# First attention: query and key norms by logarithm, exponential and a Newton step, and key norms moved into the softmax exponential

## What is computed

```python
xn = ln(x, g_norm)
q = heads(xn @ Wq)                       # 16 heads of 64
k, v = split(xn @ Wkv)                   # one head of 64, null key and value put in front
q = l2norm(q) * q_scale                  # l2norm(t) = t / max(norm(t), 1e-12)
k = l2norm(k) * k_scale
sim = q @ k.T * 8 + bias                 # bias: a small network of the relative position; causal mask
out = ln(softmax(sim) @ v @ Wout, g_out)
```

## Time and profile before

| | us |
|---|---|
| median of three runs (251.5 to 252.31) | 252.21 |
| the profiled execution | 251.66 |
| its span in the trace | 249.9 |
| GpSimd busy, 75 instructions | 58.4 |
| ScalarE busy, 178 instructions | 122.1 |
| VectorE busy, 360 instructions | 162.8 |
| TensorE busy, 1906 matmuls | 210.8 |

### The profile page before, as it was taken

The page is one execution under the profiler, slowest core; times in us unless marked ns, Lnnn a source line. Parts: engine busy times, 40 slices in busy tenths (PEclk is TensorE's granted clock), DMA queues, the critical chain, the costliest instruction groups (busy, mean ns, idle before and its releaser), DMA issues.

```text
span 249.9 us, 4768 instructions
## 1 busy us (share of the span) xinstructions
PE 210.8 (84%) x1906; PEld 141.4 (57%) x1906; DVE 162.8 (65%) x360; ACT 122.1 (49%) x178; POOL 58.4 (23%) x75
## 2 busy tenths in 40 slices
PE   0188798478897899999979989997889999999992
PEld 0154364343453464547356655764556899999992
DVE  2888779819148386889858975973953745474424
ACT  0216497677364255371634347538666542553230
POOL 3605949990000001200410027020003012000000
PEclk9999999999999999999999999999999999999997
DMA  6910055000003503400530070000000000000000
GB/s 187 422 44 0 0 146 199 4 1 0 3 0 63 129 3 107 84 0 3 116 77 0 24 155 16 0 3 0 3 3 1 4 0 21 3 21 0 21 0 21
DMA packets 10068, 11.75 MB, mean 47 GB/s; under 512 B 928, under 2 KB 9648, under 8 KB 9792
## 3 DMA queue, kind: packets, MB, share of 16 engines
q1 hardware_dynamic: 10048, 11.47, 16.5%
HBM read 10.38 MB, written 1.09 MB: 46 GB/s over the span
## 4 chain that ended last, share of the span: by engine, by line
PE 52%; DVE 27%; ACT 8%; POOL 5%; issue 4%; DMA 2%; DVEq 0%; SPq 0%; ACTq 0%
PE banks L1671 13%; PE banks L1376 6%; PE banks L1730 5%; DVE probs L958 5%; PE banks L1343 4%; PE banks L1271 3%; PE banks L1478 3%; PE banks L1396 2%; PE banks L1419 2%; PE banks L1438 2%; DMA rows<-in_rows 2%; ACT probs L594 2%; DVE zin L975 2%; ACT probs L556 2%; PE banks L1404 2%
## 5 line engine op out<-in xcount | busy, mean ns | idle before, releaser
L958 DVE TENSOR_TENSOR probs<-probs,eb 128x1024 f32<-128x1024 f32 x24 | 28.7, 1209 | 17.9 <-ACT probs L556 17.9
L594 ACT ACTIVATE probs<-banks,shift 128x1024 f32<-128x1024 f32 x24 | 25.9, 1112 | 14.9 <-PE banks L1461 14.7
L556 ACT ACTIVATE probs<-banks,key_shift 128x1024 f32<-128x1024 f32 x24 | 25.9, 1112 | 12.0 <-PE banks L1343 11.5
L1343 PE MATMUL banks<-qt,kT 64*128 64x512 f32 x96 | 25.4, 628 | 2.6 <-ACT probs L556 2.1
L1376 PE MATMUL banks<-probs,kvt 128*64 128x512 f32 (+1 forms) x128 | 23.3, 496 | 3.7 <-DVE probs L958 3.4
L363 POOL TENSOR_TENSOR qin<-qss,minus_half 128x16 f32<-128x16 f32 x8 | 23.1, 2903 | 6.4 <-DVE qss L797 6.3
L356 POOL TENSOR_TENSOR ve<-mv,ln_eps 128x2 f32<-128x2 f32 x4 | 1.7, 428 | 82.6 <-DVE mv L985 82.6
L1376 PEld LDWEIGHTS banks<-probs,kvt 128*64 128x64 f32 x128 | 7.8, 137 | 16.9 <-issue 9.7
L1671 PE MATMUL banks<-keys_space,wb 128*128 128x256 f32 (+1 forms) x72 | 17.3, 381 | 0.0
L1271 PE MATMUL banks<-wa,on 128*128 128x512 f32 x32 | 16.1, 628 | 1.2 <-DVE spread L803 1.2
L1203 DVE SCALAR_TENSOR_TENSOR x<-banks,ga,x 128x96 f32<-128x96 f32 (+1 forms) x32 | 10.2, 318 | 10.2 <-PE banks L1730 7.4
(11 more groups left out here) (214 smaller groups left out, 424.2 us busy)
## 6 DMA issues: line engine op xcount, KB each, us to landing
spread<-softmax_inverse_sums SPq DMA_DIRECT2D x16, 256.0 KB, 5.9
eb<-bias_table SPq DMA_DIRECT2D x4, 512.0 KB, 5.9
wb<-in_wb SPq DMA_DIRECT2D x1, 1842.0 KB, 10.5
wa<-in_wa SPq DMA_DIRECT2D x1, 1160.0 KB, 7.0
x<-in_x SPq DMA_DIRECT2D x1, 512.0 KB, 3.8
softmax_inverse_sums<-zin SPq DMA_DIRECT2D x4, 128.0 KB, 1.7
out<-x SPq DMA_DIRECT2D x4, 128.0 KB, 1.8
rows<-in_rows SPq DMA_DIRECT2D x1, 456.0 KB, 5.6
```

The lines of the kernel that those rows point to most:

```text
L556: nc_.activation(pb[c], sc[:, 1024 * (c % 2):1024 * (c % 2 + 1)], ACT.Exp, bias=key_shift[:, b, k:k + 1]).then_inc(s["exp_done"], 1)
L594: nc_.activation(pb[c], sc[:, 1024 * SLOT[c]:1024 * (SLOT[c] + 1)], ACT.Exp, bias=shift2[:, 3:4]).then_inc(s["exp2_done"], 1)
L958: v.tensor_tensor(p, p, w, ALU.mult).then_inc(s["mult_done"], 1)
L1343: last = mm(out.rearrange("p (m i) -> p m i", m=rhs.shape[1]), lhs, rhs, start=True, stop=True)
```

## The change

The power of -0.5 of the query tiles 3 to 7 is replaced by a logarithm and an exponential on ScalarE (`query_roots`, now there) and a Newton step of four instructions on GpSimd (`query_newton`). The key norms are made in the same way (`key_roots`, `key_newton`); the keys themselves are no longer multiplied by them: GpSimd copies the raw keys twice side by side (`keys_doubled`), and the inverse norm becomes the per-partition scale of the exponentials in `weights` and `extra_weights`. `keys_out` moves from ScalarE to VectorE. The two table loads of the stage are replaced by one, behind the last raw copy. The order of the work of all four engines is written out anew: TensorE turns the first two batches of keys ahead of query tile 5 and the other two behind the first scores, which wait for one batch instead of four, and ScalarE copies tile 7 behind the first exponential. The names of new semaphores are left out of the diff.

```diff
@@ -365,6 +366,33 @@
             def query_roots(t):
                 inverse_roots(qss[:, t], qin[:, t], "qss_ready", t, "qinv_ready")
 
+            steps = [0]
+
+            def newton(ss, root, once, done):
+
+                def then(ins):
+                    steps[0] += 1
+                    ins.then_inc(s["root_step"], 1)
+                    pool.wait_ge(s["root_step"], steps[0])
+
+                then(pool.tensor_tensor(once, root, root, ALU.mult))
+                then(pool.tensor_tensor(once, once, ss, ALU.mult))
+                then(pool.tensor_scalar(once, once, -0.5, 1.5, ALU.mult, ALU.add))
+                pool.tensor_tensor(root, root, once, ALU.mult).then_inc(s[done], 1)
+
+            def query_newton(t):
+                pool.wait_ge(s["query_roots"], t - 2)
+                pool.wait_ge(s["qinv_ready"], t)
+                newton(qss[:, t], qin[:, t], q_once[:], "qinv_ready")
+
+            def key_newton():
+                pool.wait_ge(s["key_roots"], 1)
+                newton(kss[:], kin[:], ksr[:], "kinv_ready")
+
+            def keys_doubled():
+                pool.wait_ge(s["kvt_ready"], B)
+                pool.tensor_copy(kn, kvt[:].rearrange("p b t c -> p (b t) c")[:, :, None, 0:DH].to_broadcast([P, 3 * B, 2, DH])).then_inc(s["kn_ready"], 1)
+
             def later_windows(g):
                 pool.wait_ge(s[f"windows_loaded_{g}"], 32)
                 pool.tensor_copy(eb1[:, :, 4 * g:4 * g + 4], eb0[:, :, 4 * g:4 * g + 4, 0:P]).then_inc(s["windows_copied"], 1)
@@ -378,13 +406,17 @@
                 pool.memset(buf[:], 0.0)
             pool.memset(zeros[:], 0.0).then_inc(s["cleared"], 1)
             rstd(bmv[:, :, 1], ln_eps, bve[:], brs[:], s["bias_var"], s["bias_rstd"], s["bias_pool"], 1)
-            for t in range(5):
+            for t in range(3):
                 query_roots(t)
+            keys_doubled()
+            query_newton(3)
+            query_newton(4)
+            key_newton()
+            query_newton(5)
             later_windows(0)
-            query_roots(5)
+            query_newton(6)
             later_windows(1)
-            query_roots(6)
-            query_roots(7)
+            query_newton(7)
 
             def last_normalised():
                 b = B - 1
@@ -458,18 +490,16 @@
                 nc_.activation(ksq, kvt[:].rearrange("p b t c -> p (b t) c")[:, :, 0:DH], ACT.Square).then_inc(s["ksq_ready"], 1)
 
             def key_roots():
-                nc_.preload_act_table(ACT.Sqrt)
                 act.wait_ge(s["kss_ready"], 1)
-                nc_.activation(ksr[:], kss[:], ACT.Sqrt).then_inc(s["ksr_ready"], 1)
-
-            def keys_out(b):
-                act.wait_ge(s["k_turned"], b + 1)
-                at = 512 * (b % 2)
-                nc_.activation(kT[:, b], oa[:, at:at + 2 * P], ACT.Copy, scale=qk_scale[:, 0:1])
-                for e in range(2):
-                    r = slice(DH * e, DH * (e + 1))
-                    last = nc_.activation(kx[r, b, e], oa[r, at + 2 * P:at + 2 * P + 2], ACT.Copy, scale=qk_scale[r, 0:1])
-                last.then_inc(s["kt_ready"], 1)
+                nc_.activation(kin[:], kss[:], ACT.Ln).then_inc(s["key_logs"], 1)
+                act.wait_ge(s["key_logs"], 1)
+                nc_.activation(kin[:], kin[:], ACT.Exp, scale=-0.5).then_inc(s["key_roots"], 1)
+
+            def query_roots(t):
+                act.wait_ge(s["qss_ready"], t + 1)
+                nc_.activation(qin[:, t], qss[:, t], ACT.Ln).then_inc(s["query_logs"], 1)
+                act.wait_ge(s["query_logs"], t - 2)
+                nc_.activation(qin[:, t], qin[:, t], ACT.Exp, scale=-0.5).then_inc(s["query_roots"], 1)
 
             def query_squares(t):
                 act.wait_ge(s["q_proj"], t + 1)
@@ -498,27 +528,30 @@
             keys_values_raw(2)
             keys_values_tokens(2)
             keys_values_raw(3)
+            nc_.preload_act_table_set("natural_log_exp_and_others")
             keys_values_tokens(3)
             bias_table()
             query_squares(3)
+            key_norms()
             queries_out(0)
-            key_norms()
+            query_roots(3)
             query_squares(4)
             queries_out(1)
+            query_roots(4)
+            query_squares(5)
             key_roots()
-            query_squares(5)
             queries_out(2)
-            nc_.preload_act_table_set("natural_log_exp_and_others")
+            query_roots(5)
             query_squares(6)
             queries_out(3)
+            query_roots(6)
             query_squares(7)
             queries_out(4)
             queries_out(5)
-            for b in range(B):
-                keys_out(b)
+            query_roots(7)
             queries_out(6)
-            queries_out(7)
             act.wait_ge(s["shifts"], 1)
+            act.wait_ge(s["kinv_ready"], 1)
 
             def group_read(i):
 
@@ -554,14 +587,14 @@
                     act.wait_ge(s["z_done"], 2 * b - 1 + c // 3)
                 k = c % 3 // 2
                 nc_.activation(pb[c], sc[:, 1024 * (c % 2):1024 * (c % 2 + 1)], ACT.Exp,
-                               bias=key_shift[:, b, k:k + 1]).then_inc(s["exp_done"], 1)
+                               bias=key_shift[:, b, k:k + 1], scale=kin[:, b, k:k + 1]).then_inc(s["exp_done"], 1)
 
             def extra_weights(b):
                 act.wait_ge(s["qk_x"], b + 1)
                 if b:
                     act.wait_ge(s["z_done"], 2 * b)
                 nc_.activation(px[0:2], mb[0:2, 0:32].rearrange("p (e m q) -> p e m q", e=2, m=M), ACT.Exp,
-                               bias=key_shift[0:2, b, 2:3]).then_inc(s["px_exp"], 1)
+                               bias=key_shift[0:2, b, 2:3], scale=kin[0:2, b, 2:3]).then_inc(s["px_exp"], 1)
 
             def evacuate(b, g):
                 act.wait_ge(s["pv_done"], 2 * b + g + 1)
@@ -570,6 +603,7 @@
                 nc_.copy(ob[b % 2][:, 4 * g:4 * g + 4], halves(oa, 4)).then_inc(s["o_evac"], 1)
 
             weights(0, 0)
+            queries_out(7)
             weights(0, 1)
             extra_weights(0)
             for b in range(B):
@@ -780,14 +814,14 @@
                 dve.wait_ge(s["kss_raw"], 1)
                 v.tensor_scalar(part, part, 1e-24, None, ALU.max).then_inc(s["kss_ready"], 1)
 
-            def keys_scaled():
-
-                dve.wait_ge(s["ksr_ready"], 1)
-                v.reciprocal(kin[:], ksr[:]).then_inc(s["kinv_ready"], 1)
-                dve.wait_ge(s["kinv_ready"], 1)
-                n = 3 * B
-                v.tensor_tensor(kn, kvt[:].rearrange("p b t c -> p (b t) c")[:, :, None, 0:DH].to_broadcast([P, n, 2, DH]),
-                                kin[:].rearrange("p b t -> p (b t)")[:, :, None, None].to_broadcast([P, n, 2, DH]), ALU.mult).then_inc(s["kn_ready"], 1)
+            def keys_out(b):
+                dve.wait_ge(s["k_turned"], b + 1)
+                at = 512 * (b % 2)
+                v.tensor_scalar(kT[:, b], oa[:, at:at + 2 * P], qk_scale[:, 0:1], None, ALU.mult)
+                for e in range(2):
+                    r = slice(DH * e, DH * (e + 1))
+                    last = v.tensor_scalar(kx[r, b, e], oa[r, at + 2 * P:at + 2 * P + 2], qk_scale[r, 0:1], None, ALU.mult)
+                last.then_inc(s["kt_ready"], 1)
 
             def query_sums(t):
 
@@ -882,17 +916,20 @@
             queries_scaled(1)
             query_sums(3)
             queries_scaled(2)
-            key_sums()
             query_sums(4)
             queries_scaled(3)
+            key_sums()
             query_sums(5)
             queries_scaled(4)
-            keys_scaled()
             query_sums(6)
             queries_scaled(5)
+            queries_scaled(6)
             query_sums(7)
-            queries_scaled(6)
+            keys_out(0)
+            keys_out(1)
             queries_scaled(7)
+            keys_out(2)
+            keys_out(3)
 
 
             dve.wait_ge(s["bias_loaded"], 16 * 8)
@@ -1319,9 +1356,9 @@
             turn_queries(3)
             queries(7)
             turn_queries(4)
+            turn_keys(0)
+            turn_keys(1)
             turn_queries(5)
-            for b in range(B):
-                turn_keys(b)
             turn_queries(6)
 
 
@@ -1421,8 +1458,10 @@
                 last.then_inc(s["qkv_done"], 1)
 
             pe.wait_ge(s["qt_ready"], T)
-            pe.wait_ge(s["kt_ready"], B)
+            pe.wait_ge(s["kt_ready"], 1)
             scores(0, 0)
+            turn_keys(2)
+            turn_keys(3)
             turn_queries(7)
             scores(0, 1)
             extra_scores(0)
```

More of the change, by code:

```diff
@@ L154, in adaln_ffn @@
         qin = sb("qin", [P, B * T, H])
+        q_once = sb("q_once", [P, H])
         qt = sb("qt", [P, B, M, S])
@@ L239, in adaln_ffn @@
             bias_top table_ready table_stored windows_loaded_0 windows_loaded_1 windows_copied bias_loaded
```

(4 more changed lines are left out.)

## The result

| | before | after |
|---|---|---|
| median, us (4 executions each, timed together) | 251.99 | 248.87 |
| ratio of the times, 95% interval | | 0.988 (0.986 to 0.991) |
| span of the profiled execution, us | 249.9 | 246.6 |
| first product with the values (the mark), us | 60.24 | 56.42 |

The forecast was 249.3, with 248.1 to 251.3 as its range.

The account below looks back on a forecast made before the run. Bound: a chain of waits through tile 7's root on GpSimd. Steps of -3.5 plus 0.49 give -3.0 at the mark; +0.4 after makes -2.6, 251.66 to 249.05; half-way to the median, 249.3 us; range 248.1 to 251.3.

Parts of the forecast that it names:

- to the end of tile 7's sums: VectorE's sums of query tile 7 end at 47.6 us, practically as before: -0.05 us.
- sums to scaling (the root): From tile 7's sums to its scaling, with logarithm, exponential and four GpSimd steps for a power: 3.43 to 1.8 us, -1.63.
- scaling of tile 7 to its turn: Wait for tile 7's turn on TensorE, shorter as first scores want one key batch, not four: 2.2 to 1.3 us, -0.9.
- its turn to the mark: Tile 7's turn to first product with values, first exponential and multiply done beside tile 7's copy: 7.0 to 6.05, -0.95.
- supplement for the layout: The hand-made schedule of the kernel before put the mark at 59.75, trace 60.24; this 0.49 us was added to the new one.
- mark to the end: After the first product with the values, four exponentials on the chain each 0.09 us longer: nearly +0.4 us.
- the GpSimd step: One 128x16 Newton instruction on GpSimd: estimated 0.22 us, four steps and three gaps 1.1 us; from 0.45 the gain is lost.
- the load: ScalarE's table load behind the last raw copy, 1.28 us; rival 2.66 with drain gives 250.4 to 250.7, chance 0.06 with bias table.
- the second operand: The per-partition scale added to each first-attention exponential on ScalarE: 0.09 us more each; rival with all 24 on path 0.05.
- blocked GpSimd steps: Rival: each GpSimd Newton step waits out a VectorE instruction, 1.1 us a step; time about 265 us, chance 0.04.
- The held clamp: VectorE's clamp held by a GpSimd window copy: costs up to 0.9 us of tile 6, 250 to 250.5 us.
- The multiply with the bias table: Rival: row loads start late, so VectorE's first multiply waits 1.2 us: 250.3 to 251 us, chance 0.06 with long load.

Follow-up runs that it names:

- roots_alone: The kernel before with only the new roots and the one early table load, keys multiplied on VectorE and old order kept: 254.23 us, 1.008 of the kernel before.
- newton_out: The changed kernel without the Newton steps of keys and queries: 249.46 us, 0.991 of the kernel before.
- order_better: The changed kernel with squares of tiles 4 and 6 earlier, tile 7's sums ahead of tile 6's scaling, last keys turned later: 249.87 us, 0.992 of the kernel before.
- power_kept: The changed kernel with the roots of query tiles 3 to 7 as powers on GpSimd again: 255.19 us, 1.013 of the kernel before.
- keys_first: The changed kernel with all four key batches turned ahead of tile 6 and the first scores waiting for all four: 252.01 us, 1.002 of the kernel before.

## Why the prediction was right

The steps of the sum, each from the traces of before and after, counted from the maximum over the bias table:

| step | before | after | measured | predicted |
|---|---|---|---|---|
| to the end of tile 7's sums | 18.50 | 18.54 | +0.04 | -0.05 |
| sums to scaling (the root) | 3.43 | 1.89 | -1.54 | -1.63 |
| scaling of tile 7 to its turn | 2.18 | 1.48 | -0.70 | -0.9 |
| its turn to the mark | 6.98 | 5.89 | -1.09 | -0.95 |
| supplement for the layout | | | | +0.49 |
| to the mark | 31.09 | 27.80 | -3.29 | -3.0 |
| mark to the end | 189.66 | 190.18 | +0.52 | +0.4 |

The turn of tile 7 is taken from the chain both times (53.26 in the earlier trace rows, 50.53 above). The first two steps came out within 0.1 us and the other two within 0.2, these two together within 0.1. The supplement was twice what it should have been: it took the layout to fall as far short after as before, 0.49, and after it fell short by 0.24, the sum of the four errors. All in all the traces give 2.77 less where 2.6 was forecast, and 251.66 less 2.77 is 248.89. That this is so close is in part luck, since the supplement was 0.25 too large and the stretch behind the mark 0.12 longer than forecast, and the two offset each other. That the point was put half-way to the median of before, at 249.3, can't be judged by the times: the same changed kernel had medians of 248.87 and 249.74.

The costs behind these steps held too: the GpSimd step 0.20 to 0.22 (estimate 0.22), the load 1.28 without a drain, the second operand 0.09. After the mark the estimate counted four exponentials on the path; 0.52 came, but removing the operand gave back only 0.22 there, so 0.3 of it is something else, which stays open. Of the rivals, blocked GpSimd steps had no case: none of the twenty of 128x16 was near 0.45. By the rule of the Trainium skill (GPSIMD Engine Reference, section 1, Specifications) this rival had no place in the stage; the steps agree. roots_alone shows what the move of the key multiply avoids. There the multiply, of two SBUF inputs, stays on VectorE, and a GpSimd step beside it takes 1.68 us for 0.20 and ends with it (VectorE's row, then GpSimd's):

```profile
42.62 1.75 DVE L826 TENSOR_TENSOR probs<-kvt,kin 128x1536 f32<-128x1536 f32 x1
```

```profile
42.75 1.68 POOL L380 TENSOR_SCALAR q_once<-q_once 128x16 f32<-128x16 f32 x1
```

Nothing waited for that step, but it is what the rival described. The held clamp, priced at up to 0.9, did not come up in after (46.99, 0.17 us), though it did in two of the experiments. The multiply with the bias table waited for no load: it followed VectorE's last key copy without a pause, at 52.00, 0.93 us after the end of the first exponential (49.86 + 1.21).

Two things the prediction did not see. What is late next, once the root has left the path, is TensorE's order of turns and scores together with ScalarE's copies; newton_out shows that a still shorter root gives nothing. And the gain is not a sum over parts that could be had one by one. The new roots in the old order gain nothing, and the new order with the old roots loses time, each by its own waits and then by the clock that TensorE can lose in them. The layout by hand reckons with a full clock, and the profile after has one, as in the earlier trace rows; where the clock fell, in three of the experiments, the same layout was off by 0.9 to 1.8 us. The prediction holds no word on what the new order does to the clock, so that it stayed full was luck as far as the working goes. The clock isn't the only thing that the layout can miss: for order_better it was off by 1.3 us at the full clock.

## What to carry to other kernels

Follow a late tile by hand through every engine's list to one mark, in the old and in the new order, and compare mark with mark from an event ahead of the change: that told tenths of a microsecond where the times told one. When a long serial step is shortened, ask which engine's order becomes the path, since a further shortening was worth nothing here. Read TensorE's granted clock by short stretches whenever a reordering makes it wait: work placed into those waits was worth more here than its own duration.

## What was not expected of the hardware

- **The clock falls inside a kernel's stage.** In power_kept, roots_alone and keys_first TensorE went to a granted clock of 0.50 after it had been busy 1.76 of 4 us, not at all in 2 us, and 1.90 of 4 us, and its next pieces took 1.47 to 2.08 us for 0.85 to 1.13. It came back to 1.00 as TensorE worked on. The same kernel can show the fall in one execution and not in the next (roots_alone).
- **A copy or memset on GpSimd holds a small VectorE instruction.** The clamp of 128x16 takes 0.17 us. In order_better it took 0.45 (45.59), and ended with a window copy on GpSimd (44.97 + 1.04). In newton_out it ended with a memset of 128x4096 on GpSimd, which stood earlier there than in after (44.57 + 3.52 = 48.09). VectorE of newton_out:

```profile
47.25 0.87 DVE L826 TENSOR_SCALAR qss<-qss 128x16 f32<-128x16 f32 x1
47.33 0.79 DVE L815 TENSOR_SCALAR kT<-banks,qk_scale 128x256 f32<-128x256 f32 x1
```

The key copy shown behind it waits for it (0.79, otherwise 0.48). In after the same memset runs from 50.31 to 53.83, and the key copies beside it, which read PSUM, keep their 0.48, and the first multiply with the bias table, from SBUF to SBUF, keeps its 1.23 (52.00): of these it is the clamp alone that is held. A power on GpSimd doesn't hold it (47.48, 0.17 us, inside the powers from 45.28). Without the 0.70 tile 7 of newton_out would have been scaled that much earlier still.
- **The start of the program wanders.** The maximum over the bias table began anywhere from 28.62 to 31.32 us in thirteen traces, partly for the arrival of the input rows, and this moves the whole execution.
